# Layer 1's message pass of a four-layer graph network: table in three bf16 parts, two columns a turn picked by TensorE, weights applied by ScalarE

## The chip, the cores and the metric

One core of one Trainium2 chip runs the whole program. The metric is device time in microseconds (us), lower is better; it is the median of several executions. The profile is of one more execution.

## What is computed

The input is a graph of 6250 nodes with 128 features each and 100,000 directed edges, sorted by target. Four layers of different kinds of message passing follow one another; each ends in a residual sum and a layer norm. The change touches the second one (layer 1, `_L1_gnn_ref`):

```python
src, dst = (edge_index[0], edge_index[1])
msg = edge_weight[:, None] * x[src]
agg = jax.ops.segment_sum(msg, dst, num_segments=N)
out = (1.0 + EPS) * x + agg
h = jax.nn.relu(out @ W1 + b1)
return h @ W2 + b2
```

So for each of the 100,000 edges one row of 128 float32 numbers is fetched by the edge's source node, multiplied by the edge's weight, and added to the row of its target. Layers 0, 2 and 3 do the same kind of fetch and sum with other factors.

## The kernel before

The edges are padded to 100,352 and laid out on 128 partitions with 784 columns each (`NC`). A column is 128 edges, one on each partition. The 784 columns of a partition are four strands (`STRANDS`) of 196 (`STRIDE`), so that four running sums go side by side. The function `sum_strands` works in 50 turns (`TURNS`): 48 turns of 4 steps by 4 strands, which is 16 columns, and then two turns of 8 columns. In each turn:

- GpSimd issues one indirect DMA for each column (L1103): it reads 128 indices from the tile `idx` in SBUF and fetches 128 rows of 512 bytes from the table `g.table1` in HBM into the ring `rows`. The ring holds 6 turns (`RING`). Before turn k it holds until turn k-6 has been weighed.
- One of the 16 columns of a full turn (strand 3, last step) is not fetched. `Picks` makes it from the node table `g.x`, which lies in SBUF as 50 blocks (`NB`) of 128 nodes by 128 features: TensorE broadcasts the column's source numbers to all partitions (`name`, L822, into `pcode` in PSUM), VectorE compares them with the node names of 25 blocks at a time (L813, twice in a turn: a one-hot of 3200 numbers for each partition, in the buffer `xT`, which nothing else uses yet), TensorE multiplies the 50 one-hot blocks with the 50 table blocks in float32 and adds them up in PSUM (L836; each float32 product shows as two matmul records), and ScalarE copies the sum into the ring (L847).
- VectorE waits for the DMAs of the turn (`got`), multiplies all 16 rows by their weights into `msg` (L1136 and L1137, from `rows` in SBUF and `factors` in PSUM), and then for each of the 4 steps multiplies the last sums by `keep`, which is 0 where a new target begins (L1068, into `kept` in PSUM), and adds the messages of the step (L1069).
- SyncE writes each step's sums to `prefix` in HBM (L1112), from two buffers (`ACCS`).

VectorE's order in a turn is: the two one-hots of the next turn's picked column, the wait for this turn's rows, the weighing, the four steps. TensorE does the pick of turn k, then `name` for turn k+1. `Tables2` rides along: it loads the weights of the next stages from ScalarE's queue (L1476) in turn 0 and does a few small products in turns 20 to 36. The code of the class `SplitTable` and its siblings exists only after the change.

Which operand of a VectorE instruction lies in which memory matters below. In the one-hot of L813 the first operand is in PSUM, the second in SBUF:

```python
self.code, self.found = s.ps("pcode", [P, P]), s.ps("pfound", [P, nodes.shape[2]])
```

`s.ps` allocates in PSUM, `s.sb` in SBUF. `keep`, `kept` and `factors` are in PSUM as well.

Of the kernel before, what the change touches and what calls it, by code (L numbers as in the profile page):

```python
# [5 lines left out]
P = 128  # L6
D = 128
# [5 lines left out]
NB = 50  # L13
# [31 lines left out]
class Space:  # L45


    def __init__(self, nc, name):
        self.nc, self.name, self.ctx, self.sems = nc, name, ExitStack(), []
# [23 lines left out]
    def block(self):  # L73
        return self.nc.Block()
# [57 lines left out]
def bc_last(ap, n):  # L132

    return ap.unsqueeze(2).to_broadcast([ap.shape[0], ap.shape[1], n])
# [647 lines left out]
def halved(hot):  # L782
    return [hot[:, 0:NB // 2], hot[:, NB // 2:NB]]


class Picks:
# [29 lines left out]
    def landed(self, eng, k):  # L816
        if k < self.count:
            eng.wait_ge(self.placed, k + 1)
# [192 lines left out]
def sum_strands(nc, name, g, order, table, prefix, width, weigh, aside, spot=None, acc=None):  # L1011

    with Space(nc, name) as s:
        rows = s.sb("rows", [P, RING, WIDTH, width])
        msg = s.sb("msg", [P, WIDTH, D])
        acc = s.sb("acc", [P, ACCS, WIDTH, D])[:] if acc is None else acc
        keep, kept = s.ps("keep", [P, STRIDE, STRANDS]), s.ps("kept", [P, STRANDS, D])
        idx = s.sb("idx", [P, NC], I32)  # L1020
        aside.psum(s)
        ys, us, es, weighed, summed = s.sem("ys"), s.sem("us"), s.sem("es"), s.sem("weighed"), s.sem("summed")
        indexed = s.sem("indexed")
        got = [s.sem(f"got{r}") for r in range(RING)]
        stored = [s.sem(f"sto{r}") for r in range(ACCS)]
        w = weigh(nc, s, us, es, weighed, rows, msg)
        full = sum(hi - lo == ABREAST for lo, hi in TURNS)
        picks = Picks(nc, s, g, *spot, [(STRANDS - 1) * STRIDE + TURNS[k][1] - 1 for k in range(full)]) if spot else None

        def picked(k):  # L1030
            return 1 if picks and k < picks.count else 0

        def landed(k):
            return 16 * sum(STRANDS * (TURNS[m][1] - TURNS[m][0]) - picked(m) for m in range(k % RING, k + 1, RING))

        def sums(k):
            lo, hi = TURNS[k]
            return by_strand(acc[:, k % ACCS, 0:STRANDS * (hi - lo)])

        with s.block() as block:  # L1040
            @block.vector
            def _(eng):
                v = nc.vector
                chain = Chain(eng, ys)
                aside.indices(v, chain, g, idx).then_inc(indexed, 1)
                chain.add(v.memset(acc[:, ACCS - 1], 0.0))
                chain(v.tensor_copy(keep[:], by_step(order.keep[:])))
                last = by_strand(acc[:, ACCS - 1])[:, :, ABREAST - 1]
# [24 lines left out]

            @block.tensor
            def _(pe):
                for k in range(len(TURNS)):
                    if picks:
                        picks.on_tensor(pe, k)
                    aside.on_tensor(pe, k)

            @block.scalar
            def _(act):
                if picks:
                    picks.on_scalar(act, 0, rows[:, 0, WIDTH - 1], weighed)
                for k, (lo, hi) in enumerate(TURNS):
                    aside.on_scalar(act, k)
                    w.on_scalar(act, k, STRANDS * (hi - lo))
                    if picks:
                        picks.on_scalar(act, k + 1, rows[:, (k + 1) % RING, WIDTH - 1], weighed)

            @block.gpsimd
            def _(pool):
                pool.wait_ge(indexed, 1)
                for k, (lo, hi) in enumerate(TURNS):
                    aside.on_pool(pool, k)
                    if k >= RING:
                        hold(pool, weighed, k - RING + 1)
                    for u in range(hi - lo):
                        for c in range(STRANDS):
                            j = c * STRIDE + lo + u  # L1100
                            if picked(k) and j == picks.columns[k]:
                                continue
# [1595 lines left out]
def layers1_to_3(nc, g, O, a, out):  # L2698
    with Space(nc, "l3") as t3:
        tab3 = Tables3(nc, t3, g, a)  # L2700
        with Space(nc, "l2") as s:
            base, qv = s.sb("base", [P, NC]), s.sb("qv", [P, RULES, NC])
            front = Space(nc, "l2o").__enter__()
            xT = front.sb("xT", [P, NB, D])
            wr, kn = front.sb("wr", [P, TYPES, D]), front.sb("kn", [P, NB, D])
            with Space(nc, "l2a") as q:
                tab2 = Tables2(nc, q, g, a, wr)
                sum_strands(nc, "l1z", g, O.dst, g.table1, g.prefix, D, Weighed(g.weight[:]), tab2, (g.x, halved(xT)),
                            kn[:, 0:ACCS * WIDTH].rearrange("p (c u) f -> p c u f", c=ACCS))
# [89 lines left out]
```

## Time and profile before

| what | value |
|---|---|
| median of 3 runs | 6682.17 us (6680.83 to 6683.97) |
| span of the profiled execution, first to last instruction | 6678.7 us |
| median less span | 3.5 us |
| layer 1's pass, first to last indirect DMA issue | 2389.1 to 3307.9 us |
| busy over the whole span: TensorE, VectorE, ScalarE, GpSimd | 50%, 76%, 15%, 69% |

The span is one program from the first to the last instruction; the 3.5 us are what lies around it and the difference between executions. The pass of layer 1 is 919 us of it, a good eighth. The shares over the whole span mix stages with different limits, so they say little about this pass; its own rows are below.

### The profile page before, as it was taken

The page shows a single profiled execution, that of the slowest core. Times are in us where ns is not written, and L with a number is a line of the kernel's source. Part 1 is how long each engine was busy: PE and PEld are TensorE (multiplying, and loading weights), DVE is VectorE, ACT ScalarE, POOL GpSimd, SP SyncE. Part 2 cuts the span into 40 slices and gives each one's busy share as a digit, 9 for nine tenths or more (in the row PEclk, how much of TensorE's full clock was granted, in tenths as well). Part 3 has the DMA queues.
Part 4 walks back from the last instruction along what each step waited for, and adds up shares of the span by engine and source line. Part 5 has one row for each costly group of instructions (what it writes and reads, how often), then busy time and mean ns, then how long its engine had stood idle before and what let it go on. Part 6 is the DMA issues. An engine that isn't in the chain of part 4 may idle for free. (4 is left out here: it accounts for less than half of the span.)

```text
span 6678.7 us, 61345 instructions
## 1 busy us (share of the span) xinstructions
PE 3332.5 (50%) x21638; PEld 2959.0 (44%) x21638; DVE 5046.5 (76%) x7174; ACT 1003.4 (15%) x2297; POOL 4583.7 (69%) x4753
## 2 busy tenths in 40 slices
PE   7530117467777457777468857730000004777770
PEld 5530106357777457777443327730000003777770
DVE  8999998778898677787647779986343446888886
ACT  1013333200000010000034435520000003000002
POOL 0027777677777677777667777777777767777774
PEclk9999558788989778888779988865555556888885
DMA  3036011134444344444339974433343332333332
GB/s 60 1 148 256 2 32 18 26 85 115 115 112 113 101 115 110 110 110 110 99 124 345 343 283 122 126 88 107 103 108 104 103 92 59 112 112 112 112 112 71
DMA packets 588107, 763.09 MB, mean 114 GB/s; under 512 B 118267, under 2 KB 479585, under 8 KB 568345
## 3 DMA queue, kind: packets, MB, share of 16 engines
q1 hardware_dynamic: 416916, 375.57, 17.7%
q0 software_dynamic: 152672, 272.57, 17.1%
q10 hardware_dynamic: 18210, 111.02, 4.2%
q8 instruction: 171, 2.80, 0.2%
q14 instruction: 138, 1.13, 0.1%
HBM read 346.63 MB, written 412.16 MB: 114 GB/s over the span
## 5 line engine op out<-in xcount | busy, mean ns | idle before, releaser
L1103 POOL DMA_INDIRECT l2z_rows<-proj,l2z_idx x784 | 764.5, 975 | 246.2 <-issue 238.6
L2685 POOL DMA_INDIRECT l2s_krow<-table_k,l2s_idx x762 | 721.8, 947 | 232.2 <-issue 230.4
L1103 POOL DMA_INDIRECT l0z_rows<-table,l0z_idx x736 | 697.3, 947 | 234.7 <-issue 224.0
L927 POOL DMA_INDIRECT l3z_rows<-table,l3z_idx x736 | 694.6, 944 | 234.7 <-issue 224.0
L1103 POOL DMA_INDIRECT l1z_rows<-table,l1z_idx x736 | 694.6, 944 | 233.5 <-issue 213.0
L836 PE MATMUL l3z_pfound<-l3h_hn,l3h_hot 128*128 128x130 f32 x4800 | 645.1, 303 | 233.9 <-DVE l3h_hot L813 233.9
L836 PE MATMUL l1z_pfound<-g_x,l2o_xT 128*128 128x128 f32 x4800 | 638.3, 303 | 238.9 <-DVE l2o_xT L813 238.9
L836 PEld LDWEIGHTS l3z_pfound<-l3h_hn,l3h_hot 128*128 128x128 f32 x4800 | 637.2, 218 | 241.8 <-issue 234.7
L836 PEld LDWEIGHTS l1z_pfound<-g_x,l2o_xT 128*128 128x128 f32 x4800 | 630.5, 218 | 246.6 <-issue 239.0
L2097 POOL DMA_INDIRECT first_sj<-scores,first_atdst x504 | 504.7, 1001 | 170.7 <-issue 170.7
L836 PE MATMUL l0z_pfound<-first_rows,l0r_hot 128*128 128x140 f32 x3648 | 468.0, 292 | 82.0 <-DVE l0r_hot L813 81.9
L836 PEld LDWEIGHTS l0z_pfound<-first_rows,l0r_hot 128*128 128x128 f32 x3648 | 458.0, 197 | 92.9 <-DVE l0r_hot L813 92.9
L1136 DVE TENSOR_TENSOR l2z_msg<-l2z_rows,l2z_factors 128x1024 f32<-128x1024 f32 (+1 forms) x50 | 60.0, 1200 | 511.5 <-DMA l2z_rows<-proj,l2z_idx 511.0
L2643 PE MATMUL l2s_bank<-l2o_wr,l2o_xT 128*128 128x512 f32 x800 | 373.5, 622 | 98.0 <-ACT l2s_proj L2657 83.2
L813 DVE TENSOR_TENSOR l2o_xT<-l1z_pcode,l1z_pnames 128x3200 f32<-128x3200 f32 x96 | 330.3, 3481 | 20.8 <-PE l1z_pcode L822 20.7
L813 DVE TENSOR_TENSOR l3h_hot<-l3z_pcode,l3z_pnames 128x3200 f32<-128x3200 f32 x96 | 330.4, 3483 | 12.8 <-PE l3z_pcode L822 12.5
L606 POOL IOTA sd_nidi<- 128x50 int32 x1 | 0.2, 170 | 429.8 <-POOLq L60 429.8
L2643 PEld LDWEIGHTS l2s_bank<-l2o_wr,l2o_xT 128*128 128x128 f32 x800 | 153.5, 197 | 317.7 <-issue 167.9
L899 DVE SCALAR_TENSOR_TENSOR l3z_acc<-l3z_acc,l3z_xx,l3z_msg 128x128 f32<-128x128 f32 x784 | 271.8, 347 | 25.9
L2541 PE MATMUL l2s_bank<-l2o_kn,l2o_xT 128*128 128x128 f32 x2200 | 286.2, 299 | 5.3 <-DVE l2o_xT L2522 5.3
L2541 PEld LDWEIGHTS l2s_bank<-l2o_kn,l2o_xT 128*128 128x128 f32 x2200 | 286.3, 216 | 5.5 <-issue 5.5
L268 PE MATMUL sd_turn<-g_ident,prep_key 128*128 128x128 f32 x112 | 27.5, 428 | 493.0 <-DVE prep_key L245 487.7
(619 smaller groups left out, 7639.4 us busy)
## 6 DMA issues: line engine op xcount, KB each, us to landing
proj<-l2s_proj ACTq DMA_DIRECT2D x100, 1024.0 KB
spread_q<-prep_zero SPq DMA_DIRECT2D x98, 656.0 KB
l2s_zrow<-spread_q SPq DMA_DIRECT2D x98, 656.0 KB, 4.8
prefix<-l0z_acc SPq DMA_DIRECT2D x196, 256.0 KB, 3.1
prefix<-l2o_kn SPq DMA_DIRECT2D x196, 256.0 KB
prefix<-l2z_acc SPq DMA_DIRECT2D x196, 256.0 KB
prefix<-l3z_acc SPq DMA_DIRECT2D x48, 1040.0 KB, 4.1
l2z_rows<-proj,l2z_idx POOLq DMA_INDIRECT x784, 2.6
```

Source lines behind the costliest of these rows:

```text
L268: mm = self.nc.tensor.transpose(self.turn[q][:, u], self.keys[at % 2][:, c:c + P], self.g.ident[:])
L606: nc.gpsimd.iota(nid_i[:], pattern=[[1, NB]], base=EP, channel_multiplier=NB).then_inc(numbered, 1)
L813: self.nc.vector.tensor_tensor(self.hot[i][:, 0:hi - lo], bc_mid(self.code[:], hi - lo), bc_last(self.names[:, lo:hi], P), ALU.is_equal).t ...
L836: mm = self.nc.tensor.matmul(self.found[:], self.hot[i][:, b - lo], self.nodes[:, b], start=b == 0, stop=b == NB - 1)
L899: v.scalar_tensor_tensor(acc[:, c, u, 0:D], sum_before(k, u)[:, 0:D], w.factor(k, lo, u), msg[:, u], ALU.mult, ALU.add).then_inc(summed, 1)
L927: nc.gpsimd.indirect_dma_start(out=rows[:, k % RING, u, :], out_offset=None, in_=table, in_offset=bass.IndirectOffsetOnAxis(ap=idx[:, lo + ...
L1103: nc.gpsimd.indirect_dma_start(out=rows[:, k % RING, c * (hi - lo) + u, :], out_offset=None, in_=table, in_offset=bass.IndirectOffsetOnAxi ...
L1136: chain.add(self.v.tensor_tensor(msg[:, 0:half], rows[:, 0:half], bc_last3(factor[:, 0:half], D), ALU.mult))
L2097: nc.gpsimd.indirect_dma_start(out=sj[:, j, :], out_offset=None, in_=g.scores0, in_offset=bass.IndirectOffsetOnAxis(ap=at_dst[:, j:j + 1], ...
L2541: mm = self.nc.tensor.matmul(self.found, self.hot[:, b], self.nodes[:, b], start=b == 0, stop=b == NB - 1)
L2643: mm = nc.tensor.matmul(bank[m % 2][:, b], xT[:, i, :], wr[:, c:c + wide], start=True, stop=True)
L2685: nc.gpsimd.indirect_dma_start(out=krow[:, k % KRING, c * (hi - lo) + u, :], out_offset=None, in_=g.table_k, in_offset=bass.IndirectOffset ...
```

## The change

Layer 1's pass gets a function of its own, `sum_weighed`, in place of `sum_strands` with `Weighed`. Layers 0, 2 and 3 keep theirs. What it does:

- `SplitTable` writes the node table once, at the start, as three bf16 parts whose sum is the float32 value: high = bf16(x), middle = bf16(x - high), low = x - high - middle. ScalarE makes the first two, VectorE does the subtractions, in 7 runs of at most 10 blocks. The parts lie side by side, 384 bf16 columns for a block, in space that is free during the pass.
- `SplitPicks` makes two columns of each full turn by TensorE (strands 2 and 3, last step), so that GpSimd fetches 14. The source numbers are broadcast as before; ScalarE subtracts 50 times the partition number and writes the result as bf16 to SBUF (`digit`, `shift_code`); VectorE compares it with the block numbers 0 to 49 for all 50 blocks in one instruction of 6400 bf16 numbers (`make_hot`); TensorE does 50 matmuls of 384 bf16 columns; VectorE adds up the three parts of the result with a `tensor_reduce` straight into the ring (`place`). There are two one-hot buffers and two PSUM banks.
- The weights are applied by ScalarE, in place in the ring, one instruction of 128 numbers for each column (16 in a turn), with the weight as the per-partition scale. `msg`, `factors`, L1136 and L1137 are gone. VectorE's steps wait for `weighed`, now counted by step.
- The ring slot is given back when the turn is summed, not when it is weighed.

```diff
+        self.digit = s.sb("pdigit", [P, 2, P], BF16)
+        self.places = s.sb("pplaces", [P, NB, INNER], BF16)
...
+    def on_tensor(self, pe, m):
+        t, w = self.nc.tensor, 3 * self.table.width
...
+            pe.wait_ge(self.hotted, m + 1)
+            self.name(pe, m + 2)
+            if m >= 2:
+                pe.wait_ge(self.placed, m - 1)
+            for b in range(NB):
+                mm = t.matmul(self.found[m % 2][:, 0:w], self.hot[m % 2][:, b], self.table.block(b), start=b == 0, stop=b == NB - 1)
+            mm.then_inc(self.summed, 1)
...
+            self.nc.scalar.activation(self.digit[:, m % 2], self.code(m), ACT.Identity, bias=self.shift[:, 0:1]).then_inc(self.shifted, 1)
...
+            self.nc.vector.tensor_tensor(self.hot[m % 2].rearrange("p b (c e) -> p b c e", e=INNER),
+                                         digit.unsqueeze(1).to_broadcast([P, NB, P // INNER, INNER]),
+                                         self.places[:].unsqueeze(2).to_broadcast([P, NB, P // INNER, INNER]), ALU.is_equal).then_inc(self.hotted, 1)
...
+            self.nc.vector.tensor_reduce(self.slots[m], self.found[m % 2][:, 0:3 * w].rearrange("p (t f) -> p f t", t=3), AX, ALU.add).then_inc(self.placed, 1)
```

and in `sum_weighed`, VectorE's and ScalarE's loops over the turns:

```diff
+                split.on_vector(eng, nodes, rest)
...
+                picks.make_hot(eng, 0)
+                picks.make_hot(eng, 1)
+                for m in range(2):
+                    picks.place(eng, m)
+                    picks.make_hot(eng, m + 2)
+                for k, (lo, hi) in enumerate(TURNS):
...
+                    for u in range(hi - lo):
...
+                        chain(v.tensor_tensor(kept[:], last, bc_last(keep[:, lo + u], D), ALU.mult))
+                        eng.wait_ge(weighed, lo + u + 1)
+                        v.tensor_tensor(here, kept[:], by_strand(rows[:, k % RING, 0:STRANDS * (hi - lo)])[:, :, u], ALU.add).then_inc(summed, 1)
+                        last = here
+                        if u % 2 == 0:
+                            m = 2 * k + u // 2
+                            picks.place(eng, m + 2)
+                            picks.make_hot(eng, m + 4)
...
+                    act.wait_ge(got[k % RING], landed(k))
+                    for u in range(hi - lo):
+                        if u % 2 == 0:
+                            picks.shift_code(act, 2 * k + u // 2 + 4)
+                        if u == hi - lo - 1 and k < full:
+                            act.wait_ge(picks.placed, 2 * k + 2)
+                        for c in range(STRANDS):
+                            row, j = rows[:, k % RING, c * (hi - lo) + u], c * STRIDE + lo + u
+                            ins = nc.scalar.activation(row, row, ACT.Copy, scale=weight[:, j:j + 1])
+                        ins.then_inc(weighed, 1)
```

## Rows read from the trace of the kernel before

**Rows 1.** Groups by line over the pass: busy us, mean ns | idle before, releaser
```profile
L1103 POOL DMA_INDIRECT l1z_rows<-table,l1z_idx x736 | 694.6, 944 | 233.5 <-issue 213.0 <-DVE l1z_msg L1137 11.0 <-DVE l1z_idx L764 9.5
L836 PE MATMUL l1z_pfound<-g_x,l2o_xT 128*128 128x128 f32 x4800 | 638.3, 303 | 238.9 <-DVE l2o_xT L813 238.9
L813 DVE TENSOR_TENSOR l2o_xT<-l1z_pcode,l1z_pnames 128x3200 f32<-128x3200 f32 x96 | 330.3, 3481 | 20.8 <-PE l1z_pcode L822 20.7
L1068 DVE TENSOR_TENSOR l1z_kept<-l2o_kn,l1z_keep 128x512 f32<-128x512 f32 x195 | 135.6, 695 | 10.2 <-issue 0.9
L1069 DVE TENSOR_TENSOR l2o_kn<-l1z_kept,l1z_msg 128x512 f32<-128x512 f32 x194 | 134.1, 691 | 6.6
L1136 DVE TENSOR_TENSOR l1z_msg<-l1z_rows,l1z_factors 128x1024 f32<-128x1024 f32 x48 | 58.6, 1221 | 156.2 <-DMA l1z_rows<-table,l1z_idx 156.2
```

**Rows 2.** The tile l1z_rows: duration in ns min/median/max, first and last start
```profile
L1103 POOL DMA_INDIRECT l1z_rows<-table,l1z_idx x736: 938/944/962, 2389.1 to 3307.9; - x184
```

**Rows 3.** Timeline of one turn: start, us, engine, line [idle before]
```profile
2811.69 6.88 DVE L813 TENSOR_TENSOR l2o_xT<-l1z_pcode,l1z_pnames 128x3200 f32<-128x3200 f32 x2
2812.28 0.95 POOL L1103 DMA_INDIRECT l1z_rows<-table,l1z_idx  x1 [0.30 <-issue]
2813.54 0.94 POOL L1103 DMA_INDIRECT l1z_rows<-table,l1z_idx  x1 [0.30 <-issue]
...
2815.31 14.29 PE L836 MATMUL l1z_pfound<-g_x,l2o_xT 128*128 128x128 f32 x100 [5.04 <-DVE l2o_xT L813]
```

**Rows 4.** TensorE over stretches: length, busy (instructions), granted clock, DMA share, GB/s
```profile
2839.50:2844.50 5.00, 5.00 (x47) 5.00 (x46) 1.00 0.22 56
2815.50:2820.00 4.50, 4.50 (x22) 4.50 (x23) 0.50 0.17 45
```

**Rows 5.** TensorE, bf16 counting products near the start, timeline
```profile
249.02 3.40 PE L346 MATMUL sa_ttally<-sa_tol,sa_toh 128*128 128x50 bf16 x32
```

**Rows 6.** Groups by line, whole span: bf16 compares of VectorE
```profile
L337 DVE TENSOR_TENSOR sa_toh<-prep_steps,sa_thib 128x2048 bf16<-128x2048 bf16 x49 | 59.9, 1222 | 4.3 <-PE sa_ttally L346 4.3
L338 DVE TENSOR_TENSOR sa_tol<-prep_steps,sa_tlob 128x800 bf16<-128x800 bf16 x49 | 27.9, 570 | 0.0
```

**Rows 7.** Groups by line, ScalarE in layer 2's scores
```profile
L2554 ACT ACTIVATE l2o_xT<-l2s_bank,l2s_pnames 128x128 f32<-128x128 f32 x572 | 152.2, 401 | 227.0 <-PE l2s_bank L2541 225.6 <-PE l2s_bank L2527 1.4
```

**Rows 8.** Timeline of layer 2's pass, VectorE and GpSimd
```profile
4476.70 3.42 DVE L2428 TENSOR_TENSOR l2b_bwd<-l_qv,l_attn 128x3136 f32<-128x3136 f32 x1
4477.79 3.15 POOL L1103 DMA_INDIRECT l2z_rows<-proj,l2z_idx  x1 [0.30 <-issue]
...
4490.70 1.76 DVE L2437 TENSOR_TENSOR_SCAN l2b_bwd<-l2b_same,l2b_ex 128x784 f32<-128x784 f32 x1
4491.84 1.38 POOL L1103 DMA_INDIRECT l2z_rows<-proj,l2z_idx  x1 [0.30 <-issue]
...
4503.34 3.43 DVE L2443 TENSOR_TENSOR l2b_fwd<-l2b_fwd,l2b_bwd 128x3136 f32<-128x3136 f32 x1
4503.62 3.96 POOL L1103 DMA_INDIRECT l2z_rows<-proj,l2z_idx  x1 [0.30 <-issue]
...
4519.28 19.75 DVE L2456 RECIPROCAL l2b_fwd<-l2b_fwd 128x3136 f32<-128x3136 f32 x1
4520.37 0.94 POOL L1103 DMA_INDIRECT l2z_rows<-proj,l2z_idx  x1 [0.30 <-issue]
...
4539.07 3.47 DVE L2457 TENSOR_TENSOR l2b_ex<-l2b_ex,l2b_fwd 128x3136 f32<-128x3136 f32 x1
4539.09 0.95 POOL L1103 DMA_INDIRECT l2z_rows<-proj,l2z_idx  x1 [0.30 <-issue]
4540.34 3.02 POOL L1103 DMA_INDIRECT l2z_rows<-proj,l2z_idx  x1 [0.30 <-issue]
```

**Rows 9.** Timeline of the second sort, VectorE and GpSimd
```profile
702.36 0.94 POOL L2097 DMA_INDIRECT first_sj<-scores,first_atdst  x1 [0.30 <-issue]
702.36 0.72 DVE L245 TENSOR_TENSOR prep_key<-prep_key 128x512 f32<-128x512 f32 x1
```

More of the change, by code:

```diff
@@ L1101, in _ @@
                             if picked(k) and j == picks.columns[k]:
+                                continue
+                            nc.gpsimd.indirect_dma_start(out=rows[:, k % RING, c * (hi - lo) + u, :], out_offset=None, in_=table,
+                                                         in_offset=bass.IndirectOffsetOnAxis(ap=idx[:, j:j + 1], axis=0)).then_inc(got[k % RING], 16)
+            @block.sync
+            def _(sp):
+                out = prefix[0:EP].rearrange("(p c j) f -> p c (j f)", c=STRANDS, j=STRIDE)
+                for k, (lo, hi) in enumerate(TURNS):
+                    for u in range(hi - lo):
+                        sp.wait_ge(summed, lo + u + 1)
+                        sp.dma_start(out[:, :, (lo + u) * D:(lo + u + 1) * D], sums(k)[:, :, u]).then_inc(stored[k % ACCS], 16)
+                for r in range(ACCS):
+                    sp.wait_ge(stored[r], 16 * sum(b - a for a, b in TURNS[r::ACCS]))
@@ new lines, with __init__, block, part @@
+INNER = 16
+class SplitTable:
+    def __init__(self, nc, s, width, pieces):
+        self.nc, self.width, self.where = nc, width, []
+        for ap in pieces:
+            flat = ap.bitcast(BF16)
+            count = min(flat.shape[1] // (3 * width), NB - len(self.where))
+            piece = flat[:, 0:count * 3 * width].rearrange("p (b t f) -> p b t f", t=3, f=width)
+            self.where += [(piece, b) for b in range(count)]
+        left = NB - len(self.where)
+        if left:
+            own = s.sb("split", [P, left, 3, width], BF16)
+            self.where += [(own, b) for b in range(left)]
+        self.runs = []
+        for b, (piece, at) in enumerate(self.where):
+            if self.runs and self.runs[-1][2] is piece and b - self.runs[-1][0] < SPLIT:
+                self.runs[-1][1] = b + 1
+            else:
+                self.runs.append([b, b + 1, piece, at])
+        self.high, self.rest, self.middle, self.low = (s.sem("split" + n) for n in ("high", "rest", "middle", "low"))
+    def block(self, b):
+        piece, at = self.where[b]
+        return piece[:, at].rearrange("p t f -> p (t f)")
+    def part(self, run, t):
+        lo, hi, piece, at = run
+        return piece[:, at:at + hi - lo, t]
+    def on_scalar(self, act, rows, rest):
+        c = self.nc.scalar
+        for k in range(len(self.runs) + 1):
+            if k < len(self.runs):
+                lo, hi = self.runs[k][0:2]
+                c.copy(self.part(self.runs[k], 0), rows[:, lo:hi]).then_inc(self.high, 1)
+            if k:
+                lo, hi = self.runs[k - 1][0:2]
+                act.wait_ge(self.rest, k)
+                c.copy(self.part(self.runs[k - 1], 1), rest[:, lo:hi]).then_inc(self.middle, 1)
+    def on_vector(self, eng, rows, rest):
+        v = self.nc.vector
+        for k in range(len(self.runs) + 1):
+            if k < len(self.runs):
+                lo, hi = self.runs[k][0:2]
+                eng.wait_ge(self.high, k + 1)
+                v.tensor_tensor(rest[:, lo:hi], rows[:, lo:hi], self.part(self.runs[k], 0), ALU.subtract).then_inc(self.rest, 1)
+            if k:
+                lo, hi = self.runs[k - 1][0:2]
+                eng.wait_ge(self.middle, k)
+                v.tensor_tensor(self.part(self.runs[k - 1], 2), rest[:, lo:hi], self.part(self.runs[k - 1], 1), ALU.subtract).then_inc(self.low, 1)
@@ new lines, in sum_weighed, with landed, sums, _ @@
+def sum_weighed(nc, name, g, order, table, prefix, weight, aside, spot, acc):
+    with Space(nc, name) as s:
+        nodes, hot, pieces = spot
+        rows = s.sb("rows", [P, RING, WIDTH, D])
+        split = SplitTable(nc, s, D, pieces)
+        full = sum(hi - lo == ABREAST for lo, hi in TURNS)
+        picked = {k: [c * STRIDE + TURNS[k][1] - 1 for c in (STRANDS - 2, STRANDS - 1)] for k in range(full)}
+        columns = [j for k in range(full) for j in picked[k]]
+        slots = [rows[:, k % RING, (j // STRIDE) * ABREAST + ABREAST - 1] for k in range(full) for j in picked[k]]
+        picks = SplitPicks(nc, s, g, split, [hot.bitcast(BF16)[:, h * NB * P:(h + 1) * NB * P].rearrange("p (b e) -> p b e", e=P) for h in range(2)], columns, slots)
+        kept = s.ps("kept", [P, STRANDS, D])
+        keep = s.ps("keep", [P, 1024])[:, 0:NC].rearrange("p (j c) -> p j c", c=STRANDS)
+        idx = s.sb("idx", [P, NC], I32)
+        aside.psum(s)
+        ys, weighed, summed, indexed = s.sem("ys"), s.sem("weighed"), s.sem("summed"), s.sem("indexed")
+        got = [s.sem(f"got{r}") for r in range(RING)]
+        stored = [s.sem(f"sto{r}") for r in range(ACCS)]
+        rest = hot.rearrange("p (b f) -> p b f", f=D)
+        def landed(k):
+            return 16 * sum(STRANDS * (TURNS[m][1] - TURNS[m][0]) - len(picked.get(m, [])) for m in range(k % RING, k + 1, RING))
+        def sums(k):
+            lo, hi = TURNS[k]
+            return by_strand(acc[:, k % ACCS, 0:STRANDS * (hi - lo)])
+        with s.block() as block:
+            @block.vector
+            def _(eng):
+                v = nc.vector
+                chain = Chain(eng, ys)
+                aside.indices(v, chain, g, idx).then_inc(indexed, 1)
+                chain.add(v.memset(acc[:, ACCS - 1], 0.0))
+                chain(v.tensor_copy(keep, by_step(order.keep[:])))
+                picks.start(chain)
+                split.on_vector(eng, nodes, rest)
+                last = by_strand(acc[:, ACCS - 1])[:, :, ABREAST - 1]
+                eng.wait_ge(split.low, len(split.runs))
+                eng.wait_ge(picks.set, 1)
+                picks.make_hot(eng, 0)
[3 more added lines that the diff above has]
+                    picks.make_hot(eng, m + 2)
+                for k, (lo, hi) in enumerate(TURNS):
+                    aside.on_vector(eng, chain, k)
+                    if k >= ACCS:
+                        eng.wait_ge(stored[k % ACCS], 16 * sum(b - a for a, b in TURNS[k % ACCS:k:ACCS]))
+                    for u in range(hi - lo):
+                        if lo + u:
+                            eng.wait_ge(summed, lo + u)
+                        here = sums(k)[:, :, u]
+                        chain(v.tensor_tensor(kept[:], last, bc_last(keep[:, lo + u], D), ALU.mult))
[6 more added lines that the diff above has]
+                            picks.make_hot(eng, m + 4)
+                eng.wait_ge(summed, STRIDE)
+                v.tensor_copy(g.tail[:], last)
+            @block.tensor
+            def _(pe):
+                picks.name(pe, 0)
+                picks.name(pe, 1)
+                for k in range(len(TURNS)):
+                    picks.on_tensor(pe, 2 * k)
+                    picks.on_tensor(pe, 2 * k + 1)
+                    aside.on_tensor(pe, k)
+            @block.scalar
+            def _(act):
+                split.on_scalar(act, nodes, rest)
+                for m in range(4):
+                    picks.shift_code(act, m)
+                for k, (lo, hi) in enumerate(TURNS):
+                    aside.on_scalar(act, k)
+                    act.wait_ge(got[k % RING], landed(k))
+                    for u in range(hi - lo):
+                        if u % 2 == 0:
[6 more added lines that the diff above has]
+                        ins.then_inc(weighed, 1)
+            @block.gpsimd
+            def _(pool):
+                pool.wait_ge(indexed, 1)
+                for k, (lo, hi) in enumerate(TURNS):
+                    aside.on_pool(pool, k)
+                    if k >= RING:
+                        hold(pool, summed, TURNS[k - RING][1])
+                    for u in range(hi - lo):
+                        for c in range(STRANDS):
+                            j = c * STRIDE + lo + u
+                            if j in picked.get(k, []):
@@ L2707, in layers1_to_3 @@
                 tab2 = Tables2(nc, q, g, a, wr)
-                sum_strands(nc, "l1z", g, O.dst, g.table1, g.prefix, D, Weighed(g.weight[:]), tab2, (g.x, halved(xT)),
+                spare = [kn[:, ACCS * WIDTH:NB].rearrange("p b f -> p (b f)"), qv[:].rearrange("p r j -> p (r j)"), base[:]]
+                sum_weighed(nc, "l1z", g, O.dst, g.table1, g.prefix, g.weight, tab2, (g.x, xT[:].rearrange("p b f -> p (b f)"), spare),
                             kn[:, 0:ACCS * WIDTH].rearrange("p (c u) f -> p c u f", c=ACCS))
```

43 lines of the change are left out of this document (added).

## The prediction

> **What bounds the kernel now.** I began with the groups of the pass. GpSimd is busy 694.6 us of 919 there with 736 indirect DMAs of 944 ns, and what it waits for is named "issue" nearly throughout, so nothing that another engine does [rows 1]. The view of the ring's tile says the same of single instructions: none of the 736 is longer than 962 ns [rows 2]. In the timeline they follow one another at 0.94 + 0.30 = 1.25 us [rows 3]; 735 such steps are 918.8 us, which is the pass from its first to its last issue [rows 2]. GpSimd is the bound of the pass and runs without one stop. VectorE and TensorE are the ones that wait: VectorE's weighing stood 156.2 us for the DMAs, TensorE stood 238.9 us for the one-hots [rows 1]. A turn is 15 gathers, 15 x 1.25 = 18.75 us.
>
> The reader is to see one more thing in rows 3: two one-hots of 3.44 us each run on VectorE, and the gathers beside them keep their 0.94 us. That compare reads one operand from PSUM and one from SBUF.
>
> **The change, part by part.**
>
> *Gathers.* 48 of 736 go: 48 x 1.25 = 60.0 us less work on the bounding engine. A full turn has 14, 17.5 us if nothing disturbs them.
>
> *The one-hots, VectorE.* The bf16 compares of the first stage have the same inner run of 16 as the new one and took 570 ns for 800 numbers and 1222 ns for 2048 [rows 6], so 0.522 ns a number on 0.152 us. For 6400 that is 3.50 us, two a turn, 7.0 us: as much as the two float32 ones now. The time is the same, the operands are not. `digit` and `places` both lie in SBUF; `pcode` lay in PSUM.
>
> *What two SBUF operands do to GpSimd.* Rows 8 are the rows that decide. Beside layer 2's 3136-number compares and sums with both inputs in SBUF, a gather that begins inside one takes 3.15, 3.96 or 3.02 us and not 0.94. Its end is always 0.81 to 0.82 us behind the end of the VectorE instruction (4476.70 + 3.42 = 4480.12 against 4480.94; 4506.77 against 4507.58; 4542.54 against 4543.36). The RECIPROCAL of 19.75 us with one input leaves the gather at 0.94, and a gather that begins 0.02 us behind a two-input instruction slips through with 0.95 [rows 8]. So a gather that begins inside such an instruction stands until it is over. The shape is other than in the new kernel (float32, 3136 numbers, 3.42 us, against bf16, 6400, 3.50 us), the length is all but the same.
>
> Price of one new one-hot: if the first gather begins u behind it, it ends at 3.50 + 0.82, not at u + 0.94: it is 3.38 - u late, and all gathers behind it with it. u lies between 0 and 1.25: 3.38 down to 2.13 us, 2.75 in the mean. The three measured delays are 2.21, 3.02 and 2.08, 2.44 in the mean, 2.52 with the 0.08 us that the new one is longer. I take 2.6. There are 96 one-hots, and all but the first few fall beside gathers: 96 x 2.6 = 250 us, bounds 96 x 2.13 = 204 and 96 x 3.38 = 324. The bound from the other side is no delay at all, as in rows 3; that is a rival below and not the value taken, since rows 8 match in where the operands lie and rows 3 don't.
>
> The Trainium skill, "SBUF — State Buffer", section "Who interferes with whom", says that a VectorE instruction with two SBUF inputs contends with a GpSimd instruction that reads SBUF, and that a tensor_tensor was not seen to stall DMAs because making descriptors needs only the write side, which it marks as inferred. The first half would give the loss above, the second would leave the 60 us as a gain, 6622 us. Rows 8 speak for the first half: these are DMAs whose indices lie in SBUF.
>
> *Split of the table.* VectorE subtracts 2 x 6400 float32 numbers, ScalarE converts as many, before the first pick. It is 14 instructions of VectorE, about 1.4 us each by the 695 ns for 512 numbers [rows 1], with two SBUF inputs again. Beside the scans of 1.76 us each gather took 1.38 us, one to an instruction, at a pitch of 1.68 [rows 8]; beside instructions of 1.4 us the pitch would be some 1.4, not 1.25: 14 x 0.15 = 2 us, and I put 3 (0 to 6). That VectorE comes to turn 0 some 20 us later than now costs nothing: GpSimd first needs a turn summed when it starts turn 6, over 105 us after its start.
>
> *TensorE.* At full clock 47 float32 records of 128 columns pass in 5.00 us, 106 ns each or 2 cycles of 2.4 GHz a column; at 0.50 it is 22 in 4.50 us, half the rate [rows 4]. No row has wide bf16. The bounds are 2 cycles a column as here (384 columns, 320 ns) and, with half the bytes and one record instead of two for a product, 1 cycle (160 ns). Loading 128 bf16 weights together with 50 columns took 3.40 / 32 = 106 ns [rows 5], so the load fits behind 160 ns. I take 160: 50 x 0.16 = 8.0 us and `name` 0.2, 8.2 us a pick, 16.4 a turn. After 5.04 us of idleness the burst began at granted clock 0.50 [rows 3, 4]; 5 us at half rate add 2.5 us: 18.9 us. That is below the 17.5 + 2 x 2.6 = 22.7 us that GpSimd then needs for a turn.
>
> *VectorE, sum.* 7.0 one-hots, 2 x 0.55 `place` (384 numbers, from 695 ns for 512), 4 steps of 2 x 0.73 us = 5.8, together 13.9 us; 2.4 us of weighing are gone. Covered by GpSimd. *ScalarE.* 572 activations of 128 numbers took 152.2 us together, 0.27 each [rows 7]: 16 + 2 in a turn are 4.8 us, 7.2 at the listed 401 ns. The first step of a turn waits some 1.4 us for `shift_code` and four weighings, where VectorE took 2.4 us to weigh; no loss. ScalarE and TensorE are not seen to disturb a gather.
>
> *Queues.* SyncE's stores are the same 196. ScalarE's 13 loads come after the fourth `shift_code`, in turn 0, needed in turn 20. The ring slot comes free at most a turn's steps later, with five turns of slack. The last two turns have no picks and end as now.
>
> *Sum.* -60 + 250 + 3 = +193 us. Profiled span 6678.7 + 193 = 6872; with the 3.5 us between span and median, **6875 us**. Own range: 204 - 60 = +144 to 324 - 60 + 6 = +270, 6827 to 6952.
>
> **The rivals.**
>
> *A, GpSimd isn't held and the change does what it says:* 6682 - 60 = 6622 us, plus up to 3 for the split. For it: beside the sort's compares, with both inputs in SBUF, a gather takes 0.94 us [rows 9], and a bf16 compare reads half the bytes for a number. Against it: in rows 9 gather and compare begin at the same 702.36, and the compare is 0.72 us, so two of them match one gather step and the gather may fall in a gap each time; a compare of 3.5 us leaves no such gap. The point from which it decides is a delay of 60 / 96 = 0.63 us for a one-hot; every measured one of that length is above 2. Chance 0.11. In between, delays of 0.6 to 2.1 us because only a part is held: 0.03.
>
> *B, TensorE becomes the bound.* At 320 ns a block a pick is 16.2 us, a turn 32.4 us, 13.7 over 18.75: +655 us, 7337 us. If the weight load isn't hidden, 266 ns, 13.5 us, 27.0 a turn: +396, 7078 us. It decides from (22.7 / 2 - 0.2) / 50 = 223 ns a block on. Against it: the load is hidden behind moving columns in the float32 records, where the pair also takes only 106 ns. Chance 0.05.
>
> *C, the bf16 compare runs at one number a cycle,* 6.8 us: a gather is held 6.8 - 0.1 - 0.8 = 5.9 us, 96 x 5.9 - 60 = +506, 7190 us. Against it rows 6, same inner run. Chance 0.03.
>
> **How the numbers follow.** Forecast 0.78, A 0.11, in between 0.03, B 0.05, C 0.03. The bounds of the forecast hold it nearly whole; stretched down into the case in between and a little up, 6760 to 6960 holds some 0.8. Executions of this kernel lie within 0.05%, and 0.2% (13 us) is about what a measurement can tell from no change. Faster by more: A and the lowest part of the case in between, 0.12. Within: 0.01. Slower: 0.87.
>
> **What the profile would show.** Right: gathers of layer 1 with a median still near 0.95 us but two in each turn at 3.0 to 4.3, ending 0.8 us behind a `make_hot`; a turn of about 22.7 us and a pass of some 1110 us; `make_hot` at 3.5 us; TensorE at 8 to 11 us a pick with several us idle in a turn; VectorE's steps waiting for ScalarE's weighing, and that for DMAs. Wrong: no gather over 1 us and a pass of 860 us (A); TensorE without a gap and GpSimd's idle time put down to VectorE's sums (B); `make_hot` near 6.8 us (C). What would make it wrong in size alone: a fixed phase between one-hot and gather, which settles at either end of 2.13 to 3.38 us.

## The result, and the profile after

| | before | after |
|---|---|---|
| median | 6681.5 us | 6856.06 us |
| span of the profiled execution | 6678.7 us | 6854.5 us |
| layer 1's pass, first to last indirect DMA issue | 2389.1 to 3307.9 us | 2388.1 to 3482.3 us |

The ratio is 1.0261, 95% interval 1.0248 to 1.0273: slower by 174.6 us, where 193 were forecast. The whole difference lies in the pass: 1094.2 us from first to last issue against 918.8, which is +175.4, and the spans differ by 175.8.

The groups by line over the pass of the changed kernel, to be read against [rows 1] (busy us, mean ns | idle before, releaser). In all rows POOL is GpSimd, DVE is VectorE, ACT is ScalarE, PE is TensorE's products and PEld its weight loads. A gather is one indirect DMA of GpSimd; a one-hot is the pattern of zeros and ones that `make_hot` makes by comparing, with a one where a node is the wanted one.

```profile
L1353 POOL DMA_INDIRECT l1z_rows<-table,l1z_idx x688 | 884.6, 1286 | 218.5 <-issue 208.7 <-DVE l1z_idx L764 9.2 <-DVE l2o_kn L1305 0.6
L1237 DVE TENSOR_TENSOR l2o_xT<-l1z_pdigit,l1z_pplaces 128x6400 bf16<-128x6400 bf16 x96 | 334.3, 3483 | 0.0
...
L1338 ACT ACTIVATE l1z_rows<-l1z_rows,g_weight 128x128 f32<-128x128 f32 x784 | 238.5, 390 | 42.3 <-DMA l1z_rows<-table,l1z_idx 42.3
...
L1305 DVE TENSOR_TENSOR l2o_kn<-l1z_kept,l1z_rows 128x512 f32<-128x512 f32 x196 | 135.5, 691 | 308.8 <-ACT l1z_rows L1338 303.7
...
L1245 DVE TENSOR_REDUCE l1z_rows<-l1z_pfound 128x128 f32<-128x384 f32 x96 | 53.1, 553 | 121.6 <-PE l1z_pfound L1219 121.6
```

GpSimd has 48 gathers fewer and is busy 190 us longer. Its idle time is still "issue", 0.30 us a gather: it waits for nobody between instructions. The time went into the gathers themselves, 1286 ns in the mean. 688 gathers of 944 ns would be 649.5 us; 884.6 - 649.5 = 235.1 us were spent held. With 60 us saved that is +175, the result. I use this sum, busy time less 944 ns for each gather, for every run below and call it the held time.

The tile view of the ring, to be read against [rows 2], shows that most gathers are not touched at all, while the longest takes 4.3 us:

```profile
L1353 POOL DMA_INDIRECT l1z_rows<-table,l1z_idx x688: 940/945/4266, 2388.1 to 3482.3; - x172
```

The timeline of a turn in the middle of the pass, against [rows 3]:

```profile
2914.51 3.48 DVE L1237 TENSOR_TENSOR l2o_xT<-l1z_pdigit,l1z_pplaces 128x6400 bf16<-128x6400 bf16 x1
...
2915.35 3.45 POOL L1353 DMA_INDIRECT l1z_rows<-table,l1z_idx  x1 [0.30 <-issue]
...
2919.11 0.94 POOL L1353 DMA_INDIRECT l1z_rows<-table,l1z_idx  x1 [0.30 <-issue]
...
2924.22 3.48 DVE L1237 TENSOR_TENSOR l2o_xT<-l1z_pdigit,l1z_pplaces 128x6400 bf16<-128x6400 bf16 x1
2925.34 3.18 POOL L1353 DMA_INDIRECT l1z_rows<-table,l1z_idx  x1 [0.30 <-issue]
```

One long gather to each one-hot, and its end is 0.81 to 0.82 us behind that of the compare (2914.51 + 3.48 = 2917.99 and 2915.35 + 3.45 = 2918.80; 2927.70 and 2928.52): the same figure as in [rows 8]. So it is in the whole pass: by their starts and ends in the trace 96 gathers, as many as there are one-hots, are held by a compare, each compare holding one, for 233.1 us together.

TensorE over two stretches of the same part, against [rows 4] (length, then busy time and instructions of PE, PEld, DVE, ACT, POOL, granted clock, DMA share, GB/s):

```profile
2924.00:2932.00 8.00, 8.00 (x50) 4.62 (x48) 5.70 (x5) 0.00 (x0) 6.68 (x5) 1.00 0.27 76
2914.00:2917.00 3.00, 3.00 (x11) 1.36 (x9) 3.00 (x3) 3.00 (x11) 2.59 (x2) 0.50 0.53 131
```

50 products in 8.00 us at granted clock 1.00: 160 ns for 384 bf16 columns, at 1 cycle of 2.4 GHz a column, with the weight load hidden (by their starts in the trace they are 162.5 ns apart). At 0.50 (1.2 GHz) the products begin 0.32 us apart, at 2914.15, 2914.47 and 2914.79, which is half that rate; the second row counts 11 because it takes in those that run over its edges. TensorE isn't the bound: from 2500 to 3400 us it is busy 772.5 of 900 us.

### The profile page after: what moved, and what is told of

The parts are those of the page before. It is cut to its first block and busy times, and to the rows that moved or that the text cites. A ratio compares the mean times of both kernels' runs of the same rounds, so it can differ in the third digit from the quotient of the medians.

```text
span 6854.5 us, 62591 instructions
## 1 busy us (share of the span) xinstructions
PE 3600.2 (53%) x21734; PEld 2851.6 (42%) x21734; DVE 4984.0 (73%) x7183; ACT 1263.1 (18%) x3143; POOL 4776.8 (70%) x4705
## 5 line engine op out<-in xcount | busy, mean ns | idle before, releaser
L1353 POOL DMA_INDIRECT l1z_rows<-table,l1z_idx x688 | 884.6, 1286 | 218.5 <-issue 208.7
L1103 POOL DMA_INDIRECT l2z_rows<-proj,l2z_idx x784 | 765.9, 977 | 246.1 <-issue 238.5
L1305 DVE TENSOR_TENSOR l2o_kn<-l1z_kept,l1z_rows 128x512 f32<-128x512 f32 x196 | 135.5, 691 | 308.8 <-ACT l1z_rows L1338 303.7
L813 DVE TENSOR_TENSOR l3h_hot<-l3z_pcode,l3z_pnames 128x3200 f32<-128x3200 f32 x96 | 330.3, 3482 | 12.6 <-PE l3z_pcode L822 12.6
L1237 DVE TENSOR_TENSOR l2o_xT<-l1z_pdigit,l1z_pplaces 128x6400 bf16<-128x6400 bf16 x96 | 334.3, 3483 | 0.0
L1219 PE MATMUL l1z_pfound<-l1z_split,l2o_xT 128*128 128x384 bf16 x1728 | 296.5, 326 | 0.0
L1219 PE MATMUL l1z_pfound<-l_qv,l2o_xT 128*128 128x384 bf16 x1536 | 286.9, 343 | 0.0
```

Of the source, the lines that this page charges most:

```text
L813: self.nc.vector.tensor_tensor(self.hot[i][:, 0:hi - lo], bc_mid(self.code[:], hi - lo), bc_last(self.names[:, lo:hi], P), ALU.is_equal).t ...
L1219: mm = t.matmul(self.found[m % 2][:, 0:w], self.hot[m % 2][:, b], self.table.block(b), start=b == 0, stop=b == NB - 1)
L1237: self.nc.vector.tensor_tensor(self.hot[m % 2].rearrange("p b (c e) -> p b c e", e=INNER), digit.unsqueeze(1).to_broadcast([P, NB, P // IN ...
```

## The experiments

My theory was that a gather which begins inside a VectorE instruction with two SBUF inputs stands until that instruction is over, and that this is the whole loss. Its rivals: that bf16 or the other new work (TensorE's denser products, ScalarE's 784 weighings, the later ring slot) slows GpSimd; that any long compare would do it, wherever its inputs lie; that the wait is a sharing of a port and not a wait for an end. The kernel before took 6682.5 us beside runs 1 to 4 and 6692.9 us beside runs 5 to 8, which were timed on another chip; so the ratios are compared, and the held times of the profiles. The profiled executions of runs 5 to 7 don't show these 10 us, that of run 8 does; where they come from isn't known.

**1. The kernel before, with the code in SBUF.** The only edit is that ScalarE copies the broadcast source numbers to SBUF for the float32 compares of L813:

```diff
+        self.pcode, self.code, self.broad = self.code, s.sb("pcodes", [P, P]), s.sem("pbroad")
...
+            act.wait_ge(self.broad, k + 1)
+            self.nc.scalar.copy(self.code[:], self.pcode[:]).then_inc(self.coded, 1)
...
```

> The kernel before, with one edit: ScalarE copies the broadcast source numbers from PSUM to SBUF, so that the float32 one-hot compares of layer 1 (2 x 3.44 us in a turn) have both inputs in SBUF; nothing else of the change is in it. My theory (a gather that begins inside a two-SBUF-input compare stands until that is over): per turn the first compare holds a gather 2.1 to 3.4 us and the second, right behind it, some 2.2 us, so 48 x 4.9 = +235 us, about 6915 us, with gathers of 3 to 4.2 us in the trace. Rival (it is bf16, or the heavier work of TensorE and ScalarE in the changed kernel, that slows GpSimd): no gather above 1 us and 6682 us, at most some us more for the extra copy.

Measured: 6918.22 us, ratio 1.0354 (1.0337 to 1.0371). Groups by line over the pass of this kernel, then its timeline:

```profile
L1126 POOL DMA_INDIRECT l1z_rows<-table,l1z_idx x736 | 933.6, 1268 | 233.0 <-issue 212.4 <-DVE l1z_msg L1160 11.6 <-DVE l1z_idx L764 9.1
...
L813 DVE TENSOR_TENSOR l2o_xT<-l1z_pcodes,l1z_pnames 128x3200 f32<-128x3200 f32 x96 | 330.4, 3483 | 10.9 <-ACT l1z_pcodes L864 10.9
```

```profile
2901.17 6.88 DVE L813 TENSOR_TENSOR l2o_xT<-l1z_pcodes,l1z_pnames 128x3200 f32<-128x3200 f32 x2
2901.72 3.76 POOL L1126 DMA_INDIRECT l1z_rows<-table,l1z_idx  x1 [0.30 <-issue]
...
2905.78 3.10 POOL L1126 DMA_INDIRECT l1z_rows<-table,l1z_idx  x1 [0.30 <-issue]
2909.18 0.94 POOL L1126 DMA_INDIRECT l1z_rows<-table,l1z_idx  x1 [0.30 <-issue]
```

The compares are as long as before (3483 ns against 3481 in [rows 1]) and as many; one operand has moved. 933.6 - 736 x 0.944 = 238.8 us are held, 2.49 us a compare. The instruction is float32, TensorE and ScalarE have their old work: neither bf16 nor the rest of the change is needed for the loss. All 96 compares hold one gather each, by the starts in the trace. The two compares of a turn stand back to back: the gather that begins in the first ends 0.8 us behind the first, the next one 0.8 us behind the second.

**2. The changed kernel, with the digit in PSUM.** The reverse of run 1. ScalarE writes `digit` as float32 to PSUM; one buffer in place of two, so `shift_code` waits for the one-hot before:

```diff
-        self.digit = s.sb("pdigit", [P, 2, P], BF16)
+        self.digit = s.ps("pdigit", [P, 512])[:, 0:2 * P].rearrange("p (h q) -> p h q", h=2)
...
-            if m >= 2:
-                act.wait_ge(self.hotted, m - 1)
+            if m:
+                act.wait_ge(self.hotted, m)
```

> The changed kernel with `digit` in PSUM as float32, single-buffered, so that the one-hot compare has one SBUF input. The compare then goes at one number a cycle, 6.8 us by 6400 / 0.96 plus 0.15. My theory: no gather is held (all near 0.94 us), GpSimd needs 17.5 us a turn, and VectorE is the bound with 2 x 6.8 + 1.1 + 5.8 = 20.5 us a turn: 48 x (20.5 - 18.75) = +84, 6766 us, some more for the start. Rival (the length of the compare holds GpSimd, wherever its inputs lie): two gathers a turn of 6 to 7 us, 29 us a turn, about 7190 us.

Measured: 6758.85 us, ratio 1.0117 (1.0100 to 1.0133). Groups by line over the pass, then the timeline:

```profile
L1237 DVE TENSOR_TENSOR l2o_xT<-l1z_pdigit,l1z_pplaces 128x6400 bf16<-128x6400 f32 x96 | 654.2, 6814 | 0.5 <-ACT l1z_pdigit L1229 0.5
L1353 POOL DMA_INDIRECT l1z_rows<-table,l1z_idx x688 | 651.2, 947 | 311.0 <-issue 204.6 <-DVE l2o_kn L1305 97.1 <-DVE l1z_idx L764 9.3
```

```profile
2899.79 6.81 DVE L1237 TENSOR_TENSOR l2o_xT<-l1z_pdigit,l1z_pplaces 128x6400 bf16<-128x6400 f32 x1
2899.89 0.94 POOL L1353 DMA_INDIRECT l1z_rows<-table,l1z_idx  x1 [0.30 <-issue]
...
2901.14 0.95 POOL L1353 DMA_INDIRECT l1z_rows<-table,l1z_idx  x1 [0.30 <-issue]
...
2909.84 6.81 DVE L1237 TENSOR_TENSOR l2o_xT<-l1z_pdigit,l1z_pplaces 128x6400 bf16<-128x6400 f32 x1
```

The compare is twice as long and holds nothing: 1.7 us are held in the whole pass, those of the table's split before the first turn, while 494 gathers begin inside a compare and none is held. The rival that length alone does it falls. The digit has changed its type along with its place, to float32, but the type is not what frees the gathers: the compares of run 1 are float32 too, and hold. The kernel is slower than before all the same, for another reason: GpSimd now waits 97.1 us for VectorE's sums, since VectorE has two compares of 6.81 us and is the bound; the one-hots follow each other at 10.05 us in these rows, some 20 a turn against 18.75 before.

**3. One-hots in 7 pieces of at most 8 blocks.** Operands as in the changed kernel:

```diff
+            for lo in range(0, NB, 8):
+                hi = min(lo + 8, NB)
+                ins = self.nc.vector.tensor_tensor(hot[:, lo:hi], digit.unsqueeze(1).to_broadcast([P, hi - lo, P // INNER, INNER]),
+                                                   self.places[:, lo:hi].unsqueeze(2).to_broadcast([P, hi - lo, P // INNER, INNER]), ALU.is_equal)
+            ins.then_inc(self.hotted, 1)
...
```

> The changed kernel with each one-hot made by 7 compares of at most 8 blocks (1024 numbers, about 0.69 us, one each 0.62 us) in place of one of 3.48 us; operands as in the changed kernel. My theory (a gather waits for the end of the instruction that it begins in): a gather is held 0.6 us at most, and as two compares match one gather step of 1.25 us it falls into the gaps after that: 0.1 to 0.4 us for each one-hot, -60 + 96 x 0.25 + 3 = -33, about 6650 us (6630 to 6670). VectorE needs 2 x 4.3 + 6.9 = 15.5 us a turn, still under 17.5. Rival (both share a port in proportion to the numbers read, or the whole group holds the gather): the same 2.4 us for each one-hot, 6856 us.

Measured: 6645.38 us, ratio 0.9945 (0.9928 to 0.9961). Groups by line over the pass:

```profile
L1356 POOL DMA_INDIRECT l1z_rows<-table,l1z_idx x688 | 673.9, 979 | 218.4 <-issue 208.5 <-DVE l1z_idx L764 9.1 <-DVE l2o_kn L1308 0.9
L1240 DVE TENSOR_TENSOR l2o_xT<-l1z_pdigit,l1z_pplaces 128x1024 bf16<-128x1024 bf16 x576 | 360.3, 693 | 0.0
```

24.4 us held, a tenth of 235.1, with the same numbers read from the same places. So it isn't a share of a port by what is read: the gather waits for the end of one instruction, and short ones have near ends. The change becomes a gain.

There is a second reason for so little, in the timeline of one one-hot:

```profile
2907.05 3.98 DVE L1240 TENSOR_TENSOR l2o_xT<-l1z_pdigit,l1z_pplaces 128x1024 bf16<-128x1024 bf16 x7
2907.30 1.25 POOL L1356 DMA_INDIRECT l1z_rows<-table,l1z_idx  x1 [0.30 <-issue]
2908.85 0.94 POOL L1356 DMA_INDIRECT l1z_rows<-table,l1z_idx  x1 [0.30 <-issue]
2910.10 0.94 POOL L1356 DMA_INDIRECT l1z_rows<-table,l1z_idx  x1 [0.31 <-issue]
```

The first gather is held, and the next two begin at the very time at which the fourth and the sixth piece begin (2908.85 and 2910.10 in the trace); a gather that begins together with a piece isn't held. In the whole pass 194 of the 287 gathers that begin inside a piece, or within 0.03 us of the start of one, lie within 0.03 us of a start, and only 2 of the 194 are held.

**4. One picked column a turn.** The changed kernel with strand 3 alone picked, 15 gathers and 48 one-hots:

```diff
-        picked = {k: [c * STRIDE + TURNS[k][1] - 1 for c in (STRANDS - 2, STRANDS - 1)] for k in range(full)}
+        picked = {k: [c * STRIDE + TURNS[k][1] - 1 for c in (STRANDS - 1,)] for k in range(full)}
...
```

> The changed kernel with one picked column a turn (strand 3) and 15 gathers, 48 one-hots in place of 96. My theory: no gather saved, 48 x 2.45 us of held gathers and 3 us for the split of the table: +120, about 6802 us. Rival (the loss comes from the in-place weighing or from the ring slot given back later, not from the one-hots): GpSimd's gathers 15 x 1.25 plus the same loss as before, about 6900 us, or the loss stays off the gathers' own durations.

Measured: 6797.48 us, ratio 1.0174 (1.0157 to 1.0191). The ring's gathers in the groups by line:

```profile
L1350 POOL DMA_INDIRECT l1z_rows<-table,l1z_idx x736 | 810.2, 1101 | 233.1 <-issue 211.5 <-DVE l2o_kn L1304 12.5 <-DVE l1z_idx L764 9.1
```

115.4 us held for 48 one-hots, 2.4 each, as 235.1 for 96: the loss goes by the number of one-hots. The second pick is worth -60 us of gathers and +120 us of held ones.

**5. Only the first block of a one-hot made.** From the third pick on the compare covers 128 numbers, all else stays:

```diff
+            hot = self.hot[m % 2].rearrange("p b (c e) -> p b c e", e=INNER)
+            for lo in range(0, 1 if m >= 2 else NB, 50):
+                hi = 1 if m >= 2 else NB
...
```

> The changed kernel, but from the third pick on only the first of the 50 blocks of a one-hot is made (128 numbers in place of 6400; the other blocks keep old contents); table split, TensorE's 50 products, the sums of the three parts and the weighing by ScalarE all stay. It leaves out 98% of the compares, so the picked rows are not the reference's. My theory (the loss is all the held gathers): -60 us for the 96 gathers that TensorE makes instead of 48, plus 3 to 8 for the split and the two whole compares: 6626 us (6618 to 6635). Rival (part of the loss lies in the rest of the change: TensorE's 16.4 us a turn, ScalarE's weighing, the late ring slot): above 6640 us, with GpSimd idle between gathers for more than 0.30 us.

Measured: 6637.32 us, ratio 0.9918 (0.9901 to 0.9934), that is 6627 us on 6682; profiled span 6623.7 us, 55.0 less than before. The ring's gathers:

```profile
L1356 POOL DMA_INDIRECT l1z_rows<-table,l1z_idx x688 | 655.5, 953 | 218.8 <-issue 209.4 <-DVE l1z_idx L764 9.4
```

6.0 us held, and no wait but for the index at the start. With the compares gone the change gives what 48 gathers less should give. TensorE's products, ScalarE's weighing and the later ring slot cost GpSimd nothing.

**6. One-hots in two pieces of 25 blocks.** As run 3, with 25 in place of 8.

> The changed kernel with each one-hot made by two compares of 25 blocks (3200 numbers, 1.82 us each, one each 1.75 us). My theory (held until the end of the instruction, whose end is 0.82 us before the gather's): the first compare holds a gather 1.1 us in the mean, the second about 0.5 us, 1.6 us for each one-hot: -60 + 96 x 1.6 + 3 = +97, 6779 us (6755 to 6800). Rival (only compares longer than some length hold a gather at all): 6625 us.

Measured: 6778.92 us, ratio 1.0129 (1.0112 to 1.0146), 6768 us on 6682. Groups by line, then the timeline:

```profile
L1356 POOL DMA_INDIRECT l1z_rows<-table,l1z_idx x688 | 797.9, 1160 | 218.5 <-issue 208.8 <-DVE l1z_idx L764 9.1 <-DVE l2o_kn L1308 0.6
L1240 DVE TENSOR_TENSOR l2o_xT<-l1z_pdigit,l1z_pplaces 128x3200 bf16<-128x3200 bf16 x192 | 340.8, 1817 | 0.0
```

```profile
2913.03 3.55 DVE L1240 TENSOR_TENSOR l2o_xT<-l1z_pdigit,l1z_pplaces 128x3200 bf16<-128x3200 bf16 x2
...
2914.04 1.62 POOL L1356 DMA_INDIRECT l1z_rows<-table,l1z_idx  x1 [0.30 <-issue]
...
2915.96 1.43 POOL L1356 DMA_INDIRECT l1z_rows<-table,l1z_idx  x1 [0.30 <-issue]
...
2917.69 0.94 POOL L1356 DMA_INDIRECT l1z_rows<-table,l1z_idx  x1 [0.30 <-issue]
```

148.4 us held, 1.55 for each one-hot, where 1.6 were expected. Both halves hold one gather each, as expected: 192 gathers are held by the 192 pieces. An instruction of half the length isn't free; the held time falls with the length.

**7. One-hots in ten equal pieces of 5 blocks.** As run 3, with 5 in place of 8.

> The changed kernel with each one-hot made by 10 equal compares of 5 blocks (640 numbers, about 0.49 us, one each 0.42 us, three to a gather step of 1.25 us), with no odd rest piece. The 7 compares of 8 blocks left 24 us of held gathers. My theory: a wait is at most 0.4 us and then gathers and compares run in step: some 0.12 us for each one-hot, 6682 - 60 + 12 + 3 = 6637 us (6628 to 6645), no worse than the 7 pieces. Rival (more instructions make more collisions, each with a cost of its own): 6650 us or more.

Measured: 6641.03 us, ratio 0.9923 (0.9906 to 0.9940), 6631 us on 6682; profiled span 6625.6 us. Groups by line:

```profile
L1356 POOL DMA_INDIRECT l1z_rows<-table,l1z_idx x688 | 658.6, 957 | 218.4 <-issue 207.8 <-DVE l1z_idx L764 9.1 <-DVE l2o_kn L1308 1.5
L1240 DVE TENSOR_TENSOR l2o_xT<-l1z_pdigit,l1z_pplaces 128x640 bf16<-128x640 bf16 x960 | 401.5, 489 | 0.0
```

9.1 us held, less than the 24.4 of run 3, though the intervals of the two ratios overlap. Gathers and pieces run in step here too: of the 322 gathers that begin inside a piece or within 0.03 us of a start, 202 begin within 0.03 us of a start, and 1 of those is held. VectorE pays 401.5 us for the one-hots in place of 334.3, and that is hidden: it isn't the bound. This version beats both kernels: 0.8% below the kernel before, 3.3% below the changed one (0.9923 / 1.0261 = 0.967).

**8. ScalarE's weighing alone, with the old pick.** `sum_weighed` with `Picks` in float32 in place of `SplitPicks`, no split table, 736 gathers:

```diff
-        picks = SplitPicks(nc, s, g, split, [...], columns, slots)
+        picks = Picks(nc, s, g, nodes, halved(hot.rearrange("p (b f) -> p b f", f=D)), columns)
...
+                        nc.scalar.copy(slots[k + 1], picks.found[:]).then_inc(picks.placed, 1)
```

> The other half of the change alone: ScalarE weighs in place in the ring, the ring slot is given back when its turn is summed, VectorE's two weighing instructions are gone, but the pick is the one of the kernel before (one column a turn, float32, code in PSUM, one-hots with one SBUF input, no split table). GpSimd has its 736 gathers again. My theory: no gather is held, GpSimd stays the bound, 6682 us within 5. Rival (the in-place weighing costs GpSimd time, by the ring slot or by VectorE's longer way to the end of a turn): slower by over 13 us.

Measured: 6691.66 us beside 6692.9, ratio 0.9998 (0.9988 to 1.0007). The tile view:

```profile
L1341 POOL DMA_INDIRECT l1z_rows<-table,l1z_idx x736: 941/947/965, 2391.7 to 3312.2; - x184
```

No gather above 965 ns, and the pass is 920.5 us from first to last issue against 918.8. The ratio leaves no room for the rival's 13 us: this half of the change does nothing to the time, either way.

## Why the prediction was right

**What bounds the pass.** GpSimd, before and after. Right: its idle time is "issue" in both, and every run but run 2 follows from its gathers: 60 us less where 48 are saved, and the held time, give the change of the span within 3 us (run 8 by its ratio).

**Gathers, -60 us.** Right: with the compares all but gone (run 5) the profiled span falls by 55.0 us, and 6.0 us of held time explain the rest to a us.

**Two SBUF operands.** Right, and now shown from both sides: putting the second operand into SBUF brings the loss to the kernel before (run 1), taking it out of SBUF takes the loss from the changed kernel (run 2). The reading of [rows 8] carried over from float32 sums of 3136 numbers in another stage to bf16 compares of 6400, by the length alone. [Rows 3], the compare of the same pass that the new one replaces, would have said the opposite; what they don't share is where the operands lie. The changed kernel says so once more by itself: inside its float32 sums of L1305, with `kept` in PSUM and the ring in SBUF, 145 gathers begin, and none is held. [Rows 9], which spoke for rival A, fit runs 3 and 7: beside compares of 0.7 and 0.5 us a gather is held little. The prediction's reason was that the gather falls into a gap each time. It doesn't need one: in [rows 9] gather and compare begin at the same 702.36, and runs 3 and 7 show that a gather which begins with a compare goes through.

Of the Trainium skill, "SBUF — State Buffer", section "Who interferes with whom", the rule on two SBUF inputs against a GpSimd instruction that reads SBUF holds here: 2.4 to 2.5 us held for each compare of 3.48 us (runs 1 and 4). The same section's inference that a tensor_tensor does not stall DMAs that GpSimd issues does not hold for indirect ones with their indices in SBUF. That it is the reading of the indices which waits fits this, but no run here shows which part of a gather stands.

**The size of it.** This is the term that was off: 2.6 us a one-hot. The held time less the split's 2.0 is 233.1 us, 2.43 each; 96 x 0.17 = 16 of the 18 us by which the forecast was high. I had gone between the mean of an even spread (2.75) and that of the three rows (2.52); the rows were nearer. The trace of the kernel before holds three more gathers that bear on this, which the prediction doesn't show:

```profile
4480.05 3.42 DVE L2429 TENSOR_TENSOR l2b_fwd<-l_qv,l_base 128x3136 f32<-128x3136 f32 x1
4481.25 4.16 POOL L1103 DMA_INDIRECT l2z_rows<-proj,l2z_idx  x1 [0.30 <-issue]
4483.50 1.79 DVE L2430 TENSOR_SCALAR l2b_bwd<-l2b_bwd 128x3136 f32<-128x3136 f32 x1
...
4506.80 3.42 DVE L2444 TENSOR_TENSOR l2b_fwd<-l2b_fwd,l2b_ex 128x3136 f32<-128x3136 f32 x1
4507.89 3.15 POOL L1103 DMA_INDIRECT l2z_rows<-proj,l2z_idx  x1 [0.30 <-issue]
...
4545.41 0.57 DVE L2460 TENSOR_SCALAR l_attn<-l_attn 128x784 f32<-128x784 f32 x1
4545.49 1.30 POOL L1103 DMA_INDIRECT l2z_rows<-proj,l2z_idx  x1 [0.30 <-issue]
```

The gather at 4507.89 is 2.21 us late; with it the mean is 2.38, or 2.46 with the 0.08 us, all but what was measured. The one at 4481.25 begins in the sum of L2429, but ends at 4485.41, 1.94 us behind it and 0.12 us behind the `TENSOR_SCALAR` that follows. The one at 4545.49 begins inside a `TENSOR_SCALAR` and ends 0.81 us behind it, held like the others. Both `TENSOR_SCALAR`s have one SBUF input, and the traces of all ten kernels show the same two gathers. So "always 0.81 to 0.82" left out a row, and having one SBUF input is enough for the RECIPROCAL of [rows 8] and for the sums and compares here, but not for every VectorE instruction.

The delay depends on how long behind the compare the gather begins: 0.84 and 1.12 us in the timeline above, so 2.51 and 2.24 late. In the whole pass the middle value is 1.01 us and the mean 0.93, where an even spread has 0.62. Why the phase settles there I have not tested; that the loss came within a tenth of the forecast rests in part on where it settled, since 2.13 to 3.38 us for each one-hot were open.

**Split of the table.** 3 us forecast. In the timeline of the changed kernel the 10 gathers that begin from 2393.06 to 2406.13 take 11.43 us together, 2.0 more than 10 x 0.944:

```profile
2403.79 1.22 DVE L1168 TENSOR_TENSOR l2o_xT<-g_x,l1z_split 128x1024 f32<-128x1024 f32 x1
2404.39 1.44 POOL L1353 DMA_INDIRECT l1z_rows<-table,l1z_idx  x1 [0.30 <-issue]
```

**One-hots, TensorE, ScalarE.** The bf16 compare takes 3483 ns where 3500 were worked out. A product takes 160 ns as taken, and TensorE is busy 772.5 / 900 of a turn of 22.4 us, 19.2 us where 18.9 were forecast; rival B is out, and `make_hot` at 3.5 us puts rival C out. ScalarE's weighing takes 238.5 / 784 = 0.30 us a column where I had 0.27; it is covered, as run 8 shows. A turn is (1094.2 - 20) / 48 = 22.4 us where 22.7 were forecast.

## What to carry to other kernels

Before making a VectorE instruction long, look where its inputs lie: if both are in SBUF and GpSimd is issuing indirect DMAs beside it, each such instruction costs GpSimd up to its own length (3.3 us of 3.48 at most here). Either keep one input of the tensor_tensor in PSUM, if that doesn't cost VectorE its double rate, or cut the instruction into pieces of half a microsecond, which costs VectorE some 20% more and GpSimd nearly nothing. A `TENSOR_SCALAR` holds a gather even with one SBUF input (0.57 us long, gather of 1.30 us, above), so look at the gathers beside each kind of instruction. In a profile the sign is a median duration that hasn't moved beside a mean that has, and ends that follow another engine's ends by a fixed time.

## What the runs showed of the hardware

- A gather held by a tensor_tensor with two SBUF inputs ends 0.81 to 0.82 us behind the end of that instruction, whether that is 1.2 us long (the split's subtraction), 1.8 (run 6: the first piece ends at 2914.85, the gather at 2915.66) or 3.5; behind a scan of 1.76 us it is 0.76 [rows 8]. One that begins 0.02 us behind the instruction's start slips through in 0.95 us [rows 8]; in the changed kernel one at 0.01 us does, one at 0.04 us is held.
- Held time for each one-hot of 6400 bf16 numbers, by the pieces it is cut into: 1 piece 2.4 us, 2 pieces 1.55, 7 pieces 0.25, 10 pieces 0.09 (held time by 96; the 2 us of the table's split are in it, 0.02 of each).
- A compare with one float32 input in PSUM and one bf16 input in SBUF takes 6814 ns for 6400 numbers; with both in SBUF as bf16 it takes 3483 ns. So here the operand that frees GpSimd halves VectorE's rate. Whether the place or the float32 type costs the rate isn't shown: bf16 in PSUM was not run.
